# Second attention: the reciprocal of the row sums and the maximum of the scores are moved to the head of VectorE's slot

## The reference, cut to what matters

```python
q = (draft_hidden @ Wq.T).reshape(bsz, draft_len, H, HD)          # H 16 heads, HD 128
q = _rms_norm(q, q_norm_w).transpose(0, 2, 1, 3)
kv_in = jnp.concatenate([context_hidden, draft_hidden], axis=1)   # 128 + 128 keys
k = (kv_in @ Wk.T).reshape(bsz, total_len, KVH, HD)               # KVH 4
v = (kv_in @ Wv.T).reshape(bsz, total_len, KVH, HD).transpose(0, 2, 1, 3)
k = _rms_norm(k, k_norm_w).transpose(0, 2, 1, 3)
q = _rope(q, draft_position_ids)
k = _rope(k, full_position_ids)
scores = jnp.einsum('bhqd,bhkd->bhqk', q, jnp.repeat(k, N_REP, axis=1)) * SCALE
probs = jax.nn.softmax(scores, axis=-1)
attn = jnp.einsum('bhqk,bhkd->bhqd', probs, jnp.repeat(v, N_REP, axis=1))
return attn.transpose(0, 2, 1, 3).reshape(bsz, draft_len, H * HD) @ Wo.T
```

## Time and profile before

| | |
|---|---|
| median of 3 runs | 3170.26 us (3169.36 to 3171.73) |
| profiled execution, its own time | 3171.96 us |
| span of the profiled execution | 3170.2 us |
| second attention | about 2028 to 2860 us from the span's start |
| its steady part, 13 batches | 2104 to 2747 us, 49.1 to 50.0 us per batch |

### The profile page before, as it was taken

How to read it: one execution, slowest core, us unless ns; L and a number is a source line. 1 busy time by engine, 2 the same in 40 slices (tenths; PEclk the granted TensorE clock), 3 DMA queues, 4 the chain that set the end, 5 groups by cost and what they waited for, 6 DMA issues and landing times. The chain is left out here.

```text
span 3170.2 us, 57410 instructions
## 1 busy us (share of the span) xinstructions
PE 2863.4 (90%) x16353; PEld 1637.4 (52%) x16354; DVE 1800.8 (57%) x5358; ACT 1702.8 (54%) x4566; POOL 1749.3 (55%) x2445
## 2 busy tenths in 40 slices
PE   4599999999999969999999999588898998976996
PEld 2366666666666635555555554234444444433663
DVE  4366666666666555344434445377788887862331
ACT  5578778877887623233323334266666666652331
POOL 6567777777777434455445544455566666631221
PEclk9899999999999979999999999799999999998998
DMA  6711211121112164455445547345554444547444
GB/s 240 242 42 55 77 57 47 54 77 57 47 54 81 41 217 140 135 157 157 132 140 157 157 127 215 76 89 108 107 117 106 115 113 106 117 101 280 86 84 106
DMA packets 467800, 365.79 MB, mean 115 GB/s; under 512 B 295472, under 2 KB 366128, under 8 KB 467632
## 3 DMA queue, kind: packets, MB, share of 16 engines
q1 hardware_dynamic: 404832, 285.13, 31.1%
q0 software_dynamic: 16640, 38.05, 6.1%
q10 hardware_dynamic: 46224, 41.36, 4.4%
HBM read 190.62 MB, written 115.11 MB: 96 GB/s over the span
## 5 line engine op out<-in xcount | busy, mean ns | idle before, releaser
L1415 POOL TENSOR_TENSOR e_st<-e_st,e_ws_tile 128x1024 f32<-128x1024 f32 x64 | 123.8, 1934 | 430.4 <-PE e_y L1171 419.6
L752 ACT ACTIVATE a_nrm<-a_mm,a_sc_t 128x128 f32<-128x128 f32 x768 | 291.5, 476 | 123.6 <-POOL a_sc_t L905 123.5
L603 DVE BATCH_NORM_STATS2 a_st<-a_mm 128x6 f32<-128x128 f32 x768 | 170.7, 285 | 290.3 <-PE a_mm L440 208.0
L439 PE MATMUL a_mm<-a_w_hi,a_xq_hi 128*128 128x512 f16 x768 | 297.0, 387 | 23.7 <-POOL a_xq_lo L887 15.3
L1209 ACT ACTIVATE e_hh<-e_ha 128x512 f16<-128x512 f32 x128 | 76.3, 596 | 419.5 <-PE e_ha L1156 418.0
L440 PE MATMUL a_mm<-a_w_hi,a_xq_lo 128*128 128x512 f16 x768 | 296.8, 386 | 0.0
L1304 DVE SCALAR_TENSOR_TENSOR e_hl<-e_ha,e_hh 128x512 f16<-128x512 f32 x128 | 88.5, 691 | 357.4 <-ACT e_hh L1209 357.1
L904 POOL TENSOR_TENSOR a_sc_t<-a_sc_t,a_mhalf 128x4 f32<-128x4 f32 x192 | 204.1, 1063 | 119.8 <-DVE a_sc_t L610 119.5
L1169 PE MATMUL e_y<-e_w2h,e_hh 128*128 128x512 f16 x640 | 242.6, 379 | 0.0
L1170 PE MATMUL e_y<-e_w2l,e_hh 128*128 128x512 f16 x640 | 242.6, 379 | 0.0
L1171 PE MATMUL e_y<-e_w2h,e_hl 128*128 128x512 f16 x640 | 242.6, 379 | 0.0
(11 more groups left out here) (352 smaller groups left out, 8226.9 us busy)
## 6 DMA issues: line engine op xcount, KB each, us to landing
e_st<-in_w SPq DMA_DIRECT2D x128, 512.0 KB, 4.2
disp<-a_empty SPq DMA_DIRECT2D x16, 2084.0 KB, 8.0
e_st<-in_w1b SPq DMA_DIRECT2D x32, 352.0 KB, 3.1
e_xb<-disp ACTq DMA_DIRECT2D x41, 260.5 KB, 2.7
disp<-a_empty SPq DMA_DIRECT2D x4, 2605.0 KB, 21.6
e_xb<-disp SPq DMA_DIRECT2D x40, 260.5 KB, 4.2
a_cx<-in_ctxT SPq DMA_DIRECT2D x32, 256.0 KB, 3.2
a_stage<-in_wprojT SPq DMA_DIRECT2D x16, 512.0 KB, 4.7
```

Source lines behind the costliest of these rows:

```text
L439: pe.matmul(out, xq_hi[:, n, c, :], w_hi[:, t, c, :], start=(c == 0), stop=False)
L752: ins = act.activation(nrm[:, n % 2, i * P:(i + 1) * P], src[:, i * P:(i + 1) * P], ACT.Identity, bias=sc_t[:, n % 2, 3, i:i + 1], scale=s ...
```

## The change

VectorE's list for the second attention is put into another order. No step is added or removed, and no other engine's list changes.

```diff
-            run_pipeline(dve, [("job", 2, q_low), ("in", 5, x_low), ("att", 1, smax),
-                               ("att", 3, p_low), ("att", 2, row_scale), ("job", 0, stats), ("job", 1, v_low), ("att", 5, o_low),
+            run_pipeline(dve, [("att", 2, row_scale), ("att", 1, smax), ("job", 2, q_low), ("in", 5, x_low),
+                               ("att", 3, p_low), ("job", 0, stats), ("job", 1, v_low), ("att", 5, o_low),
```

## The result

The changed kernel takes 3153.15 us (median of 4 runs, 3152.14 to 3154.37), the kernel before beside it 3170.74 us. The ratio is 0.9947, with a 95% interval of 0.9932 to 0.9963. Timed again beside other kernels it gave 3153.76 us (median of five runs; a sixth run, in a slow state, took 4379.16 us and is left out) and a ratio of 0.9949 (0.9936 to 0.9962). The forecast of 3160 us had the sign and the mechanism; the time lies at that of rival (D), for other reasons than (D) gave.

A forecast was written before the change was run, and what follows sets the result against it. TensorE was taken to wait for the exponentials of slots 3 and 5, held by chains through several engines. Terms -5.1 - 4.5 + 1.2 - 1.4 - 0.8 = -10.6 us gave 3160 us, range 3152 to 3173.

The forecast's parts named there:

- rival (D): All 0.51 us of slot 5, all 0.65 us of slot 0 in 13 batches, plus 2.2 us: -17 us, 3153 us; chance 0.04.
- (1): Slot 5: maximum ahead of `x_low` no longer holds up the exponentials; 0.51 us in ten batches, -5.1 us.
- (2): Slot 0: reciprocal ahead of `q_low` brings the normalisation 0.32 or 0.43 us earlier, six batches each, -4.5 us.
- (3): Slot 4: the query's low half, begun later, meets GpSimd's short operations; costs 0.1 us, 12 times, +1.2 us.
- (4): Slots 2, 4 and 6: reciprocal moved ahead; nearly all of `p_high`'s wait for it is cover, 0 us.
- (5): Slots 1, 3 and 7: maximum moved ahead; 0 us in steady part, -1.4 us last batch, -0.8 us other slot 1 waits.
- (6): Slot 3: `p_low` follows `q_low` at once while GpSimd's sum is pending; the sum gets its turn first, 0 us.
- rival (C): Slot 3: `p_low` keeps GpSimd from its sum, 1.66 us on the chain; +9 us, 3180 us; chance 0.09.
- Rival (B): Nothing gained: TensorE at 90% binds, not the order of independent steps; 3170 us; chance 0.10.

The follow-up runs named there:

- the fastest version: Changed kernel plus exponentials in front of the normalisation on ScalarE and `final` in front of `o_low` on VectorE: 3117.30 us, ratio 0.9826 to the kernel before.

## Why the prediction was right in kind and short in size

**What bounds.** Right: the exponentials of slots 3 and 5. A batch was to take 48.7 us and takes 48.59. TensorE was to wait 2.1 us in slot 4 and 1.7 in slot 6 (from the 2.45 and 2.17 of one batch); the means of batches 4 to 13 are 2.25 and 1.17, from 2.35 and 1.70.

**(1) The maximum in slot 5**, 0.51 us per batch: right in size. Slot 4 to slot 6 lost 0.53 us in nearly every batch, with the maximum alone as well. But it is not the maximum's own gain, since the reciprocal of slot 4 removes 0.38 us of the same wait in another way. L1714 took 1.06 us after, not the forecast 0.69: VectorE came to slot 5 earlier, the maximum started 0.39 us ahead of the sum and not behind it, and L1714 still met the sum's end.

**(2) The reciprocal in slot 0**, 0.32 or 0.43 us per batch: right in the steady part. In the one kind of batch the normalisation comes 0.27 us earlier behind the scores of slot 6 (15.16 and 14.89 us), in the other 0.46 (15.28 and 14.82), and the power in slot 0 takes 1.04 us in every batch, as forecast. About 0.30 us of it reach the scores of slot 4; the 0.39 of the means (35.71 - 35.32) contain the one batch that made up for late scores. This is the term that was mis-sized, in batches 1 and 2: their 4.0 us stand against about one in the forecast. There the reciprocal had stood inside GpSimd's sum and taken 1.02 us, and the move took it out. With the reciprocal of slot 0 alone these batches gain 2.9 us, which is 1.5 in each, and that is the part that is shown. With all reciprocals they gain 4.8 us and with the maximum alone 1.9, but there batch 0 is 1.9 us longer (48.11 us), so that batches 0 to 2 together are as before (145.93 and 145.94 us). With the change these three together have 141.14 us, in the second profile 142.72: 4.8 and 3.2 us less. I had priced the reciprocal's lead by the length of the low half (0.65 us) alone and had read no row of the first batches for it.

**(3) The price in slot 4**, 0.1 us each: it is 0. From L1978 to the start of the sum it is 2446.16 - 2441.60 = 4.56 us before and 2385.89 - 2381.34 = 4.55 after. The two short operations there only exchanged who was held up. That returns 1.2 us.

**(4) The reciprocal in slots 2, 4 and 6**, priced at nothing: the step that was wrong in its reasoning. I looked at `p_high` and what waits for it, and found cover. I did not look at what is queued behind `p_high` on ScalarE: `v_high`, for which VectorE waited 0.23 us in slot 4, and `x_high`, which `x_low` reads. They decided whether VectorE's next two-input operation met GpSimd's sum. With the reciprocal of slot 4 alone moved this is worth 5.8 us (ratio 0.9983). In the changed kernel this error costs the forecast nothing, since the maximum already had this gain. It made me expect 4 to 8 us from the reciprocal's half alone, which gave 19.3.

**(5)** The last two batches gave 2.0 us (0.78 and 1.22), where 1.4 and a share of 0.8 were forecast: right in size. TensorE's wait in front of the scores of slot 2 in the last batch fell from 2.26 to 0.85 us. It is not the maximum's alone, since the last two batches gain 2.4 us with the maximum alone and 1.6 with the reciprocal alone.

**(6) and rival (C).** Right: the sum of slot 3 took 1.45 us before and after. GpSimd goes in between `q_low` and the first of the four operations of `p_low`, which grows by 1.01 us. The kernel got faster all the same; no run takes this price out alone.

Rival (D) had the time, with 0.65 us in slot 0 in every batch; the steady part gave 0.39. The sum by parts, forecast and measured: batches 3 to 13 about 8 (ten times 0.51, eleven times 0.375, less eleven times 0.1) and 9.1 (9.5 in the second profile), batches 1 and 2 about 1 and 4.0 (4.6), the last two 1.6 and 2.0 (2.2). Batch 0 varies by more than it gains (46.19 before, 45.43 and 47.52 after).

Rival (B) read more into a page than it holds. The Trainium skill, Perfetto Trace Analysis, section Identifying the Most-Contended Engine, says to optimise the engine of the highest occupancy first, and that for TensorE the busy share of the matmuls is no good measure of how near it is to its limit; it does not say that nothing is won while every engine keeps its work. Here 17 us came from one engine's order alone with TensorE busy 90% of the span, and the fastest version, with the same work on every engine, has a ratio of 0.9826.

## What to carry to other kernels

Within a slot, put first what another engine's queue stands behind (a maximum, a reciprocal), and behind it what only a later DMA needs. Judge such a move by everything queued behind the instruction that waits, on its engine and on the next. Two orders on two engines can only be judged together: the exponentials ahead of the normalisation cost 16 us with the old list of VectorE and won 28 to 30 us with the new one, so a change tried and rejected alone deserves another try after its neighbour has moved. And read the first batches of a pipeline as well as its steady part.

## What the runs showed of the hardware

A VectorE operation with two SBUF inputs and GpSimd's sum exclude one another here, and so do the reciprocal's scaling (a `tensor_scalar`, one input in SBUF) and the sum. What it costs does not shrink with the operation: it is what is left of the sum. The scaling of 128x4 elements takes 0.17 us alone and 1.02 us inside GpSimd's sum of 128x512, and ends 0.02 us behind it. The 128x512 low half takes 0.69 us alone, 1.58 when it starts 0.24 us into the sum, 1.76 when it starts 0.05 us into it and 1.06 when it starts 0.75 us into it, and ends 0.54 to 0.56 us behind the sum each time. Between two operations of VectorE a pending GpSimd operation gets its turn: four of `p_low` took 1.66 us alone and 2.67 us with the sum pending, the first of them 1.48, and the sum's 1.45 us did not change. The Trainium skill, SBUF — State Buffer, section Who interferes with whom, says the same of the exclusion and lists `tensor_scalar` among the operations that can take the shared ports, which fits the 1.02 us. The maximum, which reads PSUM, took 1.20 to 1.23 us wherever it stood, beside the sum or not.
